# Copies of the o product out of PSUM: the odd units from ScalarE to VectorE

## What is computed

```python
# first layer: four Gaussian kernels over adj weight the rows of x
diff = (adj[..., None] - mean_relation) ** 2
w = jnp.exp(-0.5 * diff / (1e-14 + precision_relation ** 2))
w = w / jnp.sum(w, axis=-1, keepdims=True)
ws = jnp.sum(w, axis=2)
x = layernorm(x + (ws[..., None] * x[:, :, None, :]) @ W.T)   # W: 4 blocks of 128 columns
# second layer: one of four experts per batch, then the graph product
top1 = argmax(x.mean(axis=1) @ router_w + router_b)
support = x @ expert_w[top1]
out = adj @ support
# mean and variance of out over all rows of all batches of one expert
y = relu(gamma * (out - mean) / sqrt(var + 1e-5) + beta)
x = layernorm(x + y)
```

## Time and profile before

| | us |
|---|---|
| median of 3 runs | 925.3 |
| lowest, highest | 924.48, 925.61 |
| profiled execution, device time | 928.54 |
| profiled execution, span in the trace | 926.6 |
| PE busy (matmuls) | 766.6 |
| DVE busy | 783.0 |
| ACT busy | 799.0 |
| POOL busy | 633.5 |

### The profile page before, as it was taken

How to read it: one execution, slowest core, us unless ns; L and a number is a source line. 1 busy time by engine, 2 the same in 40 slices (tenths; PEclk the granted TensorE clock), 3 DMA queues, 4 the chain that set the end, 5 groups by cost and what they waited for, 6 DMA issues and landing times.

```text
span 926.6 us, 12505 instructions
## 1 busy us (share of the span) xinstructions
PE 766.6 (83%) x3922; PEld 362.6 (39%) x3922; DVE 783.0 (84%) x1702; ACT 799.0 (86%) x789; POOL 633.5 (68%) x712
## 2 busy tenths in 40 slices
PE   1445468899999999999999999999999899956652
PEld 1111123344444444444444344444444343425442
DVE  2999988999999999999999999999999712139995
ACT  4999989899999999999999999999999311139997
POOL 7499999999888888888888888888884400000000
PEclk8766679899999999999999999999999989987776
DMA  8599887888797779777877888898763003598896
GB/s 247 150 284 250 184 232 177 218 210 203 197 235 186 182 187 245 201 198 203 208 189 194 222 210 188 199 242 195 191 164 99 1 1 134 198 401 322 295 383 228
DMA packets 262676, 191.17 MB, mean 206 GB/s; under 512 B 210002, under 2 KB 210258, under 8 KB 261074
## 3 DMA queue, kind: packets, MB, share of 16 engines
q1 hardware_dynamic: 262322, 190.38, 74.8%
q10 hardware_dynamic: 288, 0.00, 0.0%
HBM read 91.52 MB, written 48.50 MB: 151 GB/s over the span
## 4 chain that ended last, share of the span: by engine, by line
DVE 49%; ACT 17%; POOL 16%; PE 10%; issue 5%; DMA 2%; SPq 0%; DVEq 0%; POOLq 0%; ACTq 0%
DVE wgt L749 19%; DVE ps_t L781 18%; DVE x_in L768 6%; PE ps_z L929 5%; ACT ps_t L530 4%; ACT ps_t L528 4%; POOL adj_cut L429 3%; PE ps_o L945 3%; POOL x_turn L440 2%; POOL adj_in L424 2%; POOL x1p L466 2%; POOL adj_cut L427 2%; ACT adjT L614 2%; PE ps_t L945 2%; DMA w_sel<-w_planes 1%
## 5 line engine op out<-in xcount | busy, mean ns | idle before, releaser
L929 PE MATMUL ps_z<-adjT,x1p 128*128 128x512 f16 x1536 | 346.5, 383 | 0.0
L914 PE MATMUL ps_h<-w0T,x_turn 128*128 128x512 f16 x768 | 196.3, 410 | 76.9 <-DVE x_in L768 54.1
L781 DVE TENSOR_TENSOR ps_t<-ps_t,wgt 128x1024 f32<-128x1024 f32 x192 | 235.9, 1229 | 15.0 <-ACT ps_t L524 10.6
L749 DVE SCALAR_TENSOR_TENSOR wgt<-wgt,ps_t 128x1024 f32<-128x1024 f32 x192 | 224.8, 1215 | 18.1 <-ACT ps_t L530 17.9
L929 PEld LDWEIGHTS ps_z<-adjT,x1p 128*128 128x128 f16 x1536 | 150.8, 99 | 183.0 <-issue 7.1
L513 ACT ACTIVATE wgt<-adj_in,neg_mu 128x1024 f32<-128x1024 f32 x192 | 205.6, 1134 | 5.5 <-issue 5.4
L519 ACT ACTIVATE wgt<-wgt 128x3072 f32<-128x3072 f32 x64 | 176.5, 2758 | 0.0
L945 PE MATMUL ps_o<-zT,w_sel 128*128 128x512 f16 x684 | 159.9, 384 | 6.2 <-DMA w_sel<-w_planes 6.1
L914 PEld LDWEIGHTS ps_h<-w0T,x_turn 128*128 128x128 f16 x768 | 76.1, 103 | 186.5 <-issue 94.0
L429 POOL TENSOR_TENSOR adj_cut<-adj_in,adj_cut 128x1024 f16<-128x1024 f32 x64 | 136.6, 2134 | 5.3
L492 POOL TENSOR_TENSOR r_nmr<-r_mv,r_std 128x4 f32<-128x4 f32 x16 | 3.2, 199 | 170.7 <-ACT r_std L607 170.7
(11 more groups left out here) (164 smaller groups left out, 864.0 us busy)
## 6 DMA issues: line engine op xcount, KB each, us to landing
adj_in<-in_adj_dram SPq DMA_DIRECT2D x64, 512.0 KB, 4.0
x_in<-in_x_dram SPq DMA_DIRECT2D x64, 256.0 KB, 4.4
x_spill<-x_in SPq DMA_DIRECT2D x28, 512.0 KB, 3.3
out_spill<-o_stage SPq DMA_DIRECT2D x49, 256.0 KB, 3.0
w_sel<-w_planes SPq DMA_DIRECT2D x8, 1024.0 KB, 6.0
adjT<-x_spill SPq DMA_DIRECT2D x6, 1024.0 KB, 9.6
out_dram<-adjT SPq DMA_DIRECT2D x6, 1024.0 KB, 12.0
adjT<-out_spill SPq DMA_DIRECT2D x4, 1024.0 KB, 9.9
```

Source lines behind the costliest of these rows:

```text
L749: v.scalar_tensor_tensor(out=wgt[:, m % 2, j, :], in0=wgt[:, m % 2, j, :], scalar=SUM_SCALE / W0_SCALE, in1=tot, op0=ALU.mult, op1=ALU.mul ...
L781: v.tensor_tensor(tot, tot, wgt[:, n % 2, j, :], ALU.add).then_inc(dve_tot, 1)
L914: last = te.matmul(ps_h[:, n % 2, :], xT[:, n % 2, left, c, :], w0T[:, right, c, :], start=(c + i == 0), stop=(c == C - 1 and i == 2))
L929: last = te.matmul(ps_z[:, u % 2, :], x1p[:, b % 2, left, t, k * P:(k + 1) * P], adjT[:, b % 2, right, t, half * HALF:(half + 1) * HALF], ...
```

## The change

For the units below KEPT, the copy out of `ps_o` is done by ACT for even u and by DVE for odd u. These are 24 odd units (1 to 47), which fall into the even turns 16 to 62. The new function `take_o` stands on DVE between `low_z` and `y_mean_var`. It is one tensor_scalar (multiply by a constant) of 128x512 from PSUM to `o_stage`, with the same three waits as ACT's copy. A new semaphore `dve_o` counts DVE's copies, and `taken(u)` names the semaphore and the count that stand for unit u; SP's store, `o_stats` and PE's next product wait for that. Units from 49 on are copied by ACT as before.

```diff
+        def taken_by_dve(u):
+            return u % 2 == 1 and u < KEPT
+
+        def taken(u):
+
+            if taken_by_dve(u):
+                return dve_o, u // 2 + 1
+            return act_o, u // 2 + 1 if u < KEPT else (KEPT + 1) // 2 + u - KEPT + 1
...
-                    sp.wait_ge(act_o, u)
+                    sp.wait_ge(*taken(u - 1))
...
-                if 0 <= u < TILES:
+                if 0 <= u < TILES and not taken_by_dve(u):
...
+            def take_o(u):
+                dve.wait_ge(pe_o, u + 1)
+                wait(dve, o_stored[1], u // 2 * 16)
+                dve.wait_ge(dve_ostat, u)
+                v.tensor_scalar(out_unit(u), ps_out(u), 1.0 / (Z_SCALE * W_SCALE), None, ALU.mult).then_inc(dve_o, 1)
+
             def o_stats(u):
                 b, half, k = u // T, u % T // G, u % G
-                dve.wait_ge(act_o, u + 1)
+                dve.wait_ge(*taken(u))
...
+                if 0 <= n - O_LAG - 1 < TILES and taken_by_dve(n - O_LAG - 1):
+                    take_o(n - O_LAG - 1)
...
-                wait(pe, act_o, u - 1 if u > KEPT + 1 else u)
+                before = u - 2 if u > KEPT + 1 else u - 1
+                if before >= 0:
+                    pe.wait_ge(*taken(before))
```

More of the change, by code:

```diff
@@ L153, in gnn_program @@
             sem(f"dve_{k}") for k in ("tot", "ws", "rest", "y", "stat", "mv"))
-        dve_z, dve_ostat, dve_omv, dve_sumT = (sem(f"dve_{k}") for k in ("z", "ostat", "omv", "sumT"))
+        dve_z, dve_o, dve_ostat, dve_omv, dve_sumT = (sem(f"dve_{k}") for k in ("z", "o", "ostat", "omv", "sumT"))
         dve_routing, dve_route, dve_alpha, dve_const = (sem(f"dve_{k}") for k in ("routing", "route", "alpha", "const"))
@@ L589, in relu @@
                 if chunks[0] == 0:
-                    wait(act, act_o, TILES if n < 2 else 0)
+                    if n < 2:
+                        act.wait_ge(*taken(TILES - 1))
                     wait(act, *landed(o_back, n))
```

## The result

The change makes the kernel slower. Its median is 935.42 us (4 runs, 934.25 to 936.98) against 925.32 us before (4 runs), 10.1 us more. The ratio is 1.0112, 95% interval 1.0093 to 1.0130. The forecast was 932.5, the range 929.8 to 935.8.

What follows compares the result with a forecast made beforehand. The prediction took a DVE and ACT ring of dependent operations as the bound. Six turns at 0.60 us, 17 at 0.21 and turn 16 at 0 gave +7.2 on 925.3, so 932.5 us, range 929.8 to 935.8.

Steps and rivals of the forecast that it cites:

- The bound and the ring: Middle stage, turns 17 to 64: additions, logarithm, exponential, row sums and weighting alternate between DVE and ACT, 10.95 us a turn.
- What the change removes is worth nothing: On ACT, 24 copies of 0.58 us go, 13.9 us in all, gaining nothing since ACT then waits for the additions.
- turn 16: First turn with a DVE copy: cost 0, since DVE's row sums waited 0.46 us there instead of 0.26.
- The step of 0.60 us: On DVE behind low_z, each added copy delays its successor by 0.60 us, bounds 0.55 and 0.70.
- The room of 0.39 us: DVE's slack before row sums while ACT computes logarithm and exponential: 0.39 us, none in turns with n mod 8 = 6.
- The sum: Over even turns 16 to 62: six at 0.60 us, 17 at 0.21, turn 16 at 0, together +7.2 us.
- What stays hidden: The later copy end delays neither PE's next o product (2.6 us of cover), SP's store, nor POOL.
- Handed through to the end: After turn 64 the delay reaches PE's last z products in full, with 1 us left either way.
- The half-time copy: Rival, 6%: DVE reads PSUM at two elements a cycle, step near 0.32 us, only 1.9 us slower, 927.2.
- The queue rival: Rival, 8%: take_o's three waits cost queue time on DVE at each copy, 2.8 us more, 935.3.
- PE's clock: Rival, 3%: longer waits before h lower PE's clock once in each batch, +10 us more, 942.7.
- ACT as the bound: Rival, 3% as faster or same: ACT's copy, not the additions, holds the logarithm; even so +0.21 us in a turn.

Runs made afterwards that it cites:

- the run with the copy first: The changed kernel with take_o moved ahead of low_z on DVE; median 934.22 us, ratio 1.0085 to the kernel before.
- the woven one: The kernel before with DVE's row-sum total and fourth weight placed between the weighting operations, solo block last, all copies on ACT; 914.96 us, ratio 0.9877.

## Why the prediction was right, and where its sum was off

**The bound and the ring.** Right. The chain of rows 2 was the limit, and ACT's copy, though level with the additions, was not in it: almost all of it taken away changed nothing, and all of it kept beside DVE's copy gave the changed kernel again.

**What the change removes is worth nothing.** Right: 10 us taken from ACT alone left every turn as it was, and in the change the time freed shows as waiting, 13.3 us. For turn 16 the forecast was wrong. Its 0 rested on rows 7, where DVE waits 0.46 us because PE's first products come late. That was a trait of the one execution: in the second profile of the kernel before DVE waits 0.25 us there and ACT not at all for PE. Turn 16 is an ordinary even turn and cost 0.28 us.

**The step of 0.60 us.** A little small. The copy moves its successor by 0.61 us, and the statistics behind it last 0.69 instead of 0.66: 0.64 to 0.65, read directly in the aggregating turns (11.67 - 11.02). I had put the overlap nearly right (0.59 in the run with the copy first) but taken the statistics' closeness into the upper bound only.

**The room of 0.39 us.** The term that was mis-sized most. I took 3.39 us from turn 46 for row sums that don't wait. There they follow the short aggregation. Behind o_stats they take 3.42 us, and the run with half the columns gives the room directly: 0.35 us. Each ordinary even turn therefore paid 0.64 - 0.35 = 0.29 us, not 0.21.

**The sum.** 17 x 0.295 = 5.0 and 6 x 0.65 = 3.9, with 0.28 of turn 16 and 0.5 of two odd turns (below), makes 9.7 us, where the trace shows 9.64. The forecast was 7.2. Its upper bound for this stage, 9.5, was passed by 0.1: it varied the step alone and took room and turn 16 as certain, and the 0.5 us of turns 29 and 49 were not in it. The total of 10.1 us lies within the stated 10.5 only by the 1 us left for the end, which was meant for something else. That part was luck.

**What stays hidden.** Right. PE's o product, SP's store and POOL show no wait for the copy between 200 and 700 us, and DVE's copy rows show no idle time before them. PE waits longer before h and POOL longer for the mean (31.2 us in all instead of 23.8), but neither stands in the chain of that stretch.

**Handed through to the end.** Right. PE's mean product behind the main loop began 15.87 us after the logarithm of turn 64 instead of 15.52 (at 749.91, with 4.32 us of waiting for POOL instead of the 3.83 in rows 8), and the slow z product after it took 7.89 instead of 8.26 us. The two about cancel.

**The rivals.** The half-time copy is out: 512 columns take 680 ns, 256 take 414, so 256 columns cost 0.27 us, 1.04 ns each. Twice that is 0.53 us for 512 elements, close to the 0.56 of the forecast and not to its half. The queue rival is out as well: no gap stands before the copy in the chain. PE's clock stayed at 1.00 between 200 and 700 us. ACT as the bound was answered by the two runs on its copies.

## To carry to other kernels

When two engines look equally busy, find the ring of dependent work between them, and ask of each operation whether the ring passes through it. An operation beside the ring costs nothing until it fills the wait of its engine, and everything above that. Taking one away pays only in turns where its engine is the bound: nothing in the kernel before, 0.11 us in each odd turn of the woven one. So price a move by the target engine's wait in each kind of turn, and look for turns that have none. And before moving work, look for latencies in the ring: weaving two short dependent operations between independent ones gave more here than any distribution of the copies.

## What the runs showed of the hardware

- The same operation, o_stats of 128x512, ran 0.66 or 0.69 us. It took 0.69, and started about 0.02 us later, where the copy that it waits for had ended just before it, with only two small operations between. It also took 0.69 behind the loop of the kernel before, where it stands idle for ACT's copies. With the copy moved further ahead it took 0.66. So a wait that isn't met yet may be enough for the longer form; no run here separates that from the data being fresh.
- A DVE operation of 128x1 with a wait on its forerunner holds the engine for about 0.19 us from start to start. Woven between independent operations, with its wait met, it costs 0.06 to 0.09 (548.72 to 548.81, 549.08 to 549.14).
- A DVE copy of 128x512 from PSUM lasts 0.68 us in its row and moves its successor by 0.59 to 0.61, since neighbours overlap.
- In the changed kernel the weighting of turn 29 started 0.35 us late and a part of that of turn 49 0.16 us late, with no releaser in the trace. The same turn 29 took 11.30 us in the run with the copy first and 11.31 in that with both copies, 10.95 in the kernel before. With half the columns, and without the aggregating turns, turn 29 took 10.95 too, and other turns were late there (34, 49 and 59, or 24). What it is stays open.
